# Raw rows one piece behind each context, values ahead of gates, two gate buffers and own columns for the squares of queries

## What is computed

```
xc = silu(causal_depthwise_conv(rmsnorm(x), 4 taps))
q, k = l2norm(xc @ wq), l2norm(xc @ wk)      16 heads of 16
v, beta, alpha = xc @ wv, sigmoid(xc @ wb), sigmoid(xc @ wa + 4)
for each token t:  S = alpha S;  S = S + k (beta (v - S k));  o = S q
h = x + o @ wo;  hn = rmsnorm(h);  x1 = h + (silu(hn @ wg) * (hn @ wu)) @ wd
cross attention of 256 queries over 120 context rows, 16 heads
mixture of 8 experts (one per token), three layers, exact GELU
```

## Time and profile before

| What | us |
|---|---|
| median of 3 runs (1851.98 to 1855.04) | 1852.46 |
| the profiled execution | 1856.45 |
| its span, first to last instruction | 1854.8 |
| VectorE busy in the span | 1229.1 |
| PE busy | 1378.5 |
| POOL busy | 1005.5 |
| ACT busy | 849.2 |

### The profile page before, as it was taken

The page is one execution under the profiler, slowest core; times in us unless marked ns, Lnnn a source line. Parts: engine busy times, 40 slices in busy tenths (PEclk is TensorE's granted clock), DMA queues, the critical chain, the costliest instruction groups (busy, mean ns, idle before and its releaser), DMA issues. The chain is left out here.

```text
span 1854.8 us, 33139 instructions
## 1 busy us (share of the span) xinstructions
PE 1378.5 (74%) x9256; PEld 1202.1 (65%) x9257; DVE 1229.1 (66%) x3269; ACT 849.2 (46%) x2808; POOL 1005.5 (54%) x1250
## 2 busy tenths in 40 slices
PE   6067748657047666565865899997499999999997
PEld 4055636436035555454654778886399999999997
DVE  3799899994988999999775143444344443443442
ACT  4332323326023675666876588887232332332332
POOL 4499789883779998999766334341112122112111
PEclk9578578859568888887977999998699999999999
DMA  5316012574121011000112111133130510511200
GB/s 131 75 41 137 17 36 59 145 169 94 63 85 33 23 34 34 22 23 27 28 34 81 54 50 45 55 121 127 37 102 24 166 34 23 166 35 47 75 17 7
DMA packets 183745, 119.32 MB, mean 64 GB/s; under 512 B 125745, under 2 KB 164584, under 8 KB 183144
## 3 DMA queue, kind: packets, MB, share of 16 engines
q1 hardware_dynamic: 119976, 90.98, 17.7%
q10 hardware_dynamic: 59248, 18.72, 4.1%
q0 software_dynamic: 4432, 8.60, 1.3%
HBM read 83.44 MB, written 35.74 MB: 64 GB/s over the span
## 5 line engine op out<-in xcount | busy, mean ns | idle before, releaser
L247 POOL TENSOR_TENSOR wt<-wt 128x1024 f32<-128x1024 f32 x128 | 301.4, 2355 | 72.4 <-DVE wt L192 51.4
L253 POOL TENSOR_TENSOR wt<-wt 128x512 f32<-128x512 f32 (+2 forms) x384 | 304.4, 793 | 30.1
L1972 PE MATMUL e_ph<-e_g,e_w 128*128 128x128 f32 x2496 | 285.2, 276 | 0.7 <-ACT e_g L1942 0.7
L1972 PEld LDWEIGHTS e_ph<-e_g,e_w 128*128 128x128 f32 x2496 | 281.9, 192 | 0.9 <-issue 0.9
L192 DVE SCALAR_TENSOR_TENSOR wt<-wt,scan 128x256 f32<-128x256 f32 x512 | 242.9, 474 | 1.8 <-POOL wt L247 1.8
L171 DVE TENSOR_REDUCE wt<-wt 128x16 f32<-128x272 f32 x512 | 220.2, 430 | 0.1
L182 DVE TENSOR_TENSOR scan<-wt,scan 128x256 f32<-128x256 f32 x512 | 215.9, 422 | 0.3
L160 DVE TENSOR_TENSOR wt<-wt,scan 128x256 f32<-128x256 f32 x512 | 211.0, 412 | 0.9 <-PEq L270 0.5
L1450 ACT ACTIVATE wt<-p_pX,p_mx 128x120 f32<-128x120 f32 x512 | 176.4, 387 | 75.8 <-DVE p_mx L1235 75.6
L1933 ACT ACTIVATE e_g<-e_ph,wt 128x128 f32<-128x128 f32 x156 | 48.7, 363 | 305.0 <-PE e_ph L1972 305.0
L1851 POOL TENSOR_TENSOR e_ve<-e_mv,eps 128x1 f32<-128x1 f32 x39 | 7.4, 189 | 330.8 <-DVE e_mv L1907 330.8
(11 more groups left out here) (229 smaller groups left out, 2884.9 us busy)
## 6 DMA issues: line engine op xcount, KB each, us to landing
wt<-in_L_ffn_W SPq DMA_DIRECT2D x24, 1024.0 KB, 5.2
qkv<-f_st ACTq DMA_DIRECT2D x48, 256.0 KB, 2.6
p_kE<-kE SPq DMA_DIRECT2D x16, 480.0 KB, 3.7
p_vP<-vP SPq DMA_DIRECT2D x16, 480.0 KB, 4.6
wt<-qkv SPq DMA_DIRECT2D x12, 512.0 KB, 5.3
e_xt<-routed ACTq DMA_DIRECT2D x39, 130.0 KB, 2.1
f_xt<-in_x SPq DMA_DIRECT2D x32, 128.0 KB, 2.9
p_oT<-o SPq DMA_DIRECT2D x16, 256.0 KB, 2.8
```

What stands on the lines that cost most here:

```text
L247: nc.gpsimd.tensor_tensor(x, s["S"][:, h, z * Q:(z + 1) * Q], s["qn"][:, h, z * Q:(z + 1) * Q].rearrange("p t (o d) -> p t o d", o=1).to_b ...
L253: nc.gpsimd.tensor_tensor(x[:, :, :, 0:half], x[:, :, :, 0:half], x[:, :, :, half:2 * half], ALU.add).then_inc(s["o_fold"][h], 1)
L1972: ins = nc.tensor.matmul(ph2[:, c // 2, c % 2], w2[:, s, i, c * P:(c + 1) * P], g1[:, i], start=(i == 0), stop=(i == C1 - 1))
```

## The change

Five edits, all in `front_and_scan`:

- `bst` gets two slots by the unit's parity, with a semaphore each; a copy of gates waits for the store of two units before.
- `load_raw` loads values ahead of gates, and can load one of the four pieces alone.
- In the loop over contexts, the four whole `load_raw` behind contexts 2, 4, 6, 8 become 16 pieces, one behind each of steps 1 to 16: keys, queries, values, gates of part 2 half 0, then part 3 half 0, part 2 half 1, part 3 half 1.
- Where the span is 64 columns (parts 0 and 1), the squares of queries get columns 64 to 127 of `squares`, and keys keep 0 to 63; ACT then waits for the sums of the half before only.
- `with_lengths` takes places among the 16 steps of two chunks: behind steps 6, 8, 9, 12, 14, 15 for part 1 and 5, 8, 9, 11, 14, 15 for parts 2 and 3, where it was 4, 6, 7, 12, 14, 15 for both.

```diff
-        bst = sb("bst", [48, 4, PT])
+        bst = sb("bst", [48, 2, 4, PT])
...
+        plane = lambda i, n: squares[:, :, i * n:(i + 1) * n] if 2 * n <= TB else squares[:, :, 0:n]
...
-                for i, name, dst in ((1, "k", x["k"]), (0, "q", x["q"]), (3, None, None), (2, "v", x["vo"])):
+                for i, name, dst in ((1, "k", x["k"]), (0, "q", x["q"]), (2, "v", x["vo"]), (3, None, None))[some.start:some.stop]:
                     if i == 3:
                         later = part > 0
-                        sp.wait_ge(gates_out[later], 128 * (units - U * later))
+                        for slot in range(2):
+                            sp.wait_ge(gates_out[later][slot], 64 * (units - U * later))
...
-            later = {2 + 2 * i: (2 + i % 2, i // 2) for i in range(4)}
+            later = {1 + i: (2 + i // 4 % 2, i // 8, range(i % 4, i % 4 + 1)) for i in range(16)}
...
                 def sums(i):
                     folds = (p * 2 + i) * 4
                     dve.wait_ge(sq_done, p * 2 + i + 1)
+                    x = plane(i, n)
...
-                        dst = squares[:, 0:half, 0:n] if half > 1 else lens[:, h, i:i + 1, 0:n]
-                        nc.vector.tensor_tensor(dst, squares[:, 0:half, 0:n], squares[:, half:2 * half, 0:n], ALU.add).then_inc(fold_done, 1)
+                        dst = x[:, 0:half] if half > 1 else lens[:, h, i:i + 1, 0:n]
+                        nc.vector.tensor_tensor(dst, x[:, 0:half], x[:, half:2 * half], ALU.add).then_inc(fold_done, 1)
...
-            def with_lengths(some, c, last=False):
-
-                for h in range(2):
-                    parts = list(lengths(some, h))
-                    for u in range(R):
-                        scan_step(nc, dve, s, 0, c + h, u, last=last and h == 1)
-                        if u in (4, 6, 7):
-                            parts.pop(0)()
+            def with_lengths(some, c, places, last=False):
+
+                parts = [*lengths(some, 0), *lengths(some, 1)]
+                for u in range(2 * R):
+                    scan_step(nc, dve, s, 0, c + u // R, u % R, last=last and u >= R)
+                    if u in places:
+                        parts[places.index(u)]()
...
-            with_lengths(1, CHUNKS // 2 - 3)
+            with_lengths(1, CHUNKS // 2 - 3, (6, 8, 9, 12, 14, 15))
...
-            with_lengths(2, CHUNKS - 2, last=True)
+            with_lengths(2, CHUNKS - 2, (5, 8, 9, 11, 14, 15), last=True)
...
-                if n == U:
-                    act.wait_ge(gates_out[0], n * 128)
-                elif n >= 1:
-                    act.wait_ge(gates_out[n > U], (n - U * (n > U)) * 128)
-                nc.scalar.activation(bst[:].rearrange("p b t -> p (b t)"), pp[0:48, 3, 0], ACT.Copy).then_inc(evac_done, 1)
+                if n >= 2:
+                    later = n - 2 >= U
+                    act.wait_ge(gates_out[later][n % 2], ((n - 2 - U * later) // 2 + 1) * 128)
+                nc.scalar.activation(bst[:, n % 2].rearrange("p b t -> p (b t)"), pp[0:48, 3, 0], ACT.Copy).then_inc(evac_done, 1)
...
-                    if p < 2 and (p or i):
-                        act.wait_ge(fold_done, (p * 2 + i) * 4)
-                    elif p == 2 and i == 0:
-                        act.wait_ge(fold_done, 16)
-                    elif p >= 2:
+                    if p in (1, 2):
+                        act.wait_ge(fold_done, ((p - 1) * 2 + i + 1) * 4)
+                    elif p == 3:
+                        act.wait_ge(lens_done, summed(p - 1, i))
+                    elif p > 3:
                         act.wait_ge(lens_done, summed(p, i) - 1)
-                    nc.scalar.activation(squares[:, :, 0:n], src[:, h, :, now], ACT.Square).then_inc(sq_done, 1)
+                    nc.scalar.activation(plane(i, n), src[:, h, :, now], ACT.Square).then_inc(sq_done, 1)
...
-                        ins = nc.tensor.matmul(squared[:, i, 0:n], ident[:], squares[:, d, 0:n], start=(d == 0), stop=(d == HD - 1))
+                        ins = nc.tensor.matmul(squared[:, i, 0:n], ident[:], plane(i, n)[:, d], start=(d == 0), stop=(d == HD - 1))
```

More of the change, by code:

```diff
@@ L317, in front_and_scan @@
         out = [sem(f"f_out_{n}") for n in "qkv"]
-        gates_out = [sem(f"f_gates_out{i}") for i in range(2)]
+        gates_out = [[sem(f"f_gates_out{i}{slot}") for slot in range(2)] for i in range(2)]
         (ss_done, rstd_done, xn_done, T_done, tail_done, xT_done, conv_done, xc_done, proj_done, evac_done) = (
@@ L349, in store_gates @@
                         eng.dma_start(k["gates"][i, n, a, g].rearrange("q h t -> h q t"),
-                                      bst[32 * i + g * H // G:32 * i + (g + 1) * H // G, 2 * a:2 * a + 2]).then_inc(gates_out[n >= U], 16)
+                                      bst[32 * i + g * H // G:32 * i + (g + 1) * H // G, n % 2, 2 * a:2 * a + 2]).then_inc(gates_out[n >= U][n % 2], 16)
         @block.sync
@@ L371, in load_weights, with load_raw @@
                     sp.dma_start(bv[:], row(w["L0_xattn_bv"], 1)).then_inc(small_in, 16)
-            def load_raw(part, h):
+            def load_raw(part, h, some=range(4)):
                 units = U * part + U // 2 * (h + 1)
```

## The result

The changed kernel takes 1829.59 us (median of 4 runs, 1825.32 to 1832.96) against 1853.44 for the kernel before (4 runs on the same chip): a ratio of 0.988, with a 95% interval of 0.9861 to 0.9899. That is 23.9 us, 1.3%, faster. The profiled execution took 1832.96 us, its span is 1831.3.

The account below looks back on a forecast made before the run. VectorE's scan and its two waits for ACT's sigmoid were taken to bound the first stage. Gains of 3.6 + 5.9 + 20.2 = 29.7 us off 1856.45 gave 1826.7, less 4.0 for the median 1822.7; range 1817 to 1834, about 0.8.

Parts of the forecast that it names:

- the forecast's band of 1 to 7: VectorE's second wait for gates: 1 to 7 us left, time 1821 to 1827, chance 0.40.
- Rival 4: First-stage gains do not reach the end, as something else holds the barrier or second stage: 1852.5 us, chance 0.04.
- Start: Ahead of VectorE's scan: second gates buffer and own columns for squares start it 3.6 us earlier, bounds 5.5 and -1.
- The 1.5 us charged for values ahead of gates: SP's loads ahead of the scan: gates going behind the values costs about 1.5 us again.
- First stall: VectorE's 5.93 us wait for part 1's sigmoid: own columns or later place alone covers it; 5.9 gained, bounds 5 and 5.9.
- Second stall: VectorE's 23.16 us wait at gates of parts 2 and 3: 20.2 us gained, 3 left; bounds 23.2 and 3.
- 20.6 us saved: Loop of sixteen contexts ends at 420.0 instead of 440.6; 26 saved at PE's fast pace, 14 at the slow.
- contexts over in 75 to 82 us: A sign that would show the forecast: ACT's sixteen contexts last 75 to 82 us.
- Rival 1: Both VectorE stalls vanish and the scan alone bounds the first stage: 32.7 us gained, 1819.8, chance 0.33.
- the sum's last line: 29.7 us off the profiled execution's 1856.45 gives 1826.7; the median lies 4.0 below the profiled one, so 1822.7.
- Rival 2: Context loop hardly shortens; second stall keeps 8 to 20 us, gain 12.5 to 24.7, time 1828 to 1840, chance 0.19.
- Rival 3: Context loop becomes serial, each load waiting for its piece: about 161 us instead of 96.3, time 1905, chance 0.04.

Follow-up runs that it names:

- shared_columns: Changed kernel with squares of queries in the keys' columns again, with the waits this needs, new places kept; 1829.41 us.
- late_place: Changed kernel with VectorE's parts for parts 2 and 3 behind steps 8, 10, 11, 13, 14, 15; 1822.94 us.
- warm_pe: Changed kernel with eight more PE products of 128 columns behind each context, whose result nobody reads; 1824.09 us.
- changed_again: The changed kernel without an edit, run and profiled a second time; 1829.75 us.
- gates_first: Changed kernel with gates loaded ahead of values in every group again; 1828.86 us.
- spread_alone: Kernel before with only the raw-row pieces spread one by one over the contexts, gates still ahead of values; 1840.96 us against 1854.21.
- part2_early: Changed kernel with part 2's raw rows loaded behind units 13 and 14, leaving eight pieces of part 3 in the context loop; 1825.32 us.

## Why the prediction was right, and where its terms were off

It said faster, 1822.7 us, 1817 to 1834; measured were 1829.59, inside the range and 6.9 above the number. A stall of 6.5 and 5.3 us is in the forecast's band of 1 to 7; the median is not in its 1821 to 1827. Point by point:

- **That VectorE's chain arrives whole at the barrier** holds: 26.95 us at the barrier from 4.11 + 5.93 + 16.65 = 26.7 at the three places. The 396.2 to 398.8 us of scan show it for every run. Rival 4, that the time doesn't reach the end, is out.
- **Start, 3.6 us:** 4.11, and 2.6 to 4.2 over the eight profiles. The second buffer brings it, as the term said; own columns, in the same term, bring nothing (60.84 in `shared_columns` too). The 1.5 us charged for values ahead of gates were 0.5 in this profile, no more than the spread.
- **First stall, 5.9 us:** 5.93. "Either alone covers" it is half wrong. The places alone do; the columns alone leave 2.74 us at the roots, which the step left at two steps behind the gates without asking what was late next.
- **Second stall, 20.2 us gained:** 16.65, and 17.9 in the second execution. This is the mis-sized term, and in it the loop's length: "20.6 us saved" from a pace between PE's two; it was 13.3, near the figure for the slow pace, and 17.3 in the second. (That figure is given as 14; its own steps, 9 x 5.5 + 3 x 4.8 = 63.9, make it 15.1. And 23.16 - 2.96 - 20.6 + 1.8 + 0.9 leaves 2.3 us, where 3 were taken.) The row that it was built on showed a granted clock of 0.71, and the changed loop has 0.75 over its length; the slow end was the one nearest to the row. The rest came out as charged or better: the place and the later arrival gave 5.0 us (2.96 expected; the contexts start 12.9 us sooner, VectorE comes to its place only 7.9 sooner), and the sums on PE and sigmoid cost 1.6 more (1.8). By these, 23.2 - 5.0 - 13.3 + 1.6 = 6.5. The sign "contexts over in 75 to 82 us" was missed by the first execution (83.1) and met by the second (79.1).
- **Rival 1**, no stall left, 1819.8: this is what `late_place` and `warm_pe` are, 1822.94 and 1824.09. So some 3 us of the miss seem to lie outside the stalls, in the sum's last line; in the changed kernel, too, the three places give 26.7 us and the medians 22.9 to 23.9. It took a gain read from one execution off the median of others. The profiled pair, before and `late_place`, differs by 31.7 us (1856.45 - 1824.77), near the 32.7 that the rival's sum gives; the medians by 29.5. The profiled execution of before lay 4.0 above its median, and part of that was, it seems, in the very stalls that the sum took out. That was not tried by itself.
- **Rival 2**, that the loop hardly shortens, is wrong in its reason (13 to 17 us shorter), though its lower edge, 8 us of stall, lay near.
- **Rival 3**, the serial loop of 161 us, did not come: SP issued the next load ahead of the stores, and the loop took 83.1. By the same row a context load does stand behind its piece: the median landing is 4.9 us, against 4.7 with a piece and 2.9 without.

PE's waits for context loads were to spread "over a dozen contexts of 1 to 3 us each". They are still 8, up to 4.7, with a sum of 19.7 instead of 35.1; the sum fell by 15.4, and the loop by 13.3. In these waits PE stands idle, and behind the one of 4.22 us shown above the granted clock was 0.50, where it was 1.00 ahead of it. The Trainium skill (TensorE: Matmul & The Clock Gate, section HAM oscillation — how this bites in real kernels) tells of a kernel whose groups of products are shorter than the wait for their data, so that each starts slow. The trace agrees at that wait, 2.8 us of products and 4.22 of waiting; but only 8 of the 16 contexts have a wait. Over 60 us of the loop the clock was 0.72 with the waits, and 1.00 when the gaps were filled.

What stays open: why the same loop took 83.1 us in one execution and 79.1 in another, and 76.8 to 83.7 where the edits lay elsewhere. Of the nine profiles with the pieces spread one by one and no added products, the shortest loop has the highest granted clock, 0.81 (above), and the longest the lowest, 0.71, `shared_columns`:

```profile
331.90:415.60 83.70, 65.41 (x254) 46.54 (x254) 83.70 (x258) 36.47 (x113) 73.44 (x75) 0.71 0.74 180
```

In between the two do not go together: 0.75 with 83.1 us in the changed kernel, 0.76 with 79.1 in `changed_again`, and 0.77 with 83.5 in `gates_first` and in `spread_alone`, the two with gates ahead of values. That a higher clock shortens the loop is shown by `warm_pe`; what sets the clock one way or the other from one execution to the next was not found.

## What to carry to other kernels

A wait that stops the bounding engine can be hidden by asking later: three more scan steps ahead of it did as much as a supplier that is done sooner (`part2_early`); the scan ended at 458.9 and 457.4 where it was 463.4, and with both together no sooner, at 457.8. The first takes one line. Before a wait is removed, ask what the same engine needs next; here it was the roots. And bulk loads that share a queue with small ones that a loop needs each step go one behind each step: the same bytes, in pieces, made the loop 13 us shorter.

## What the runs showed that was not expected

- Adding work to PE made a loop faster: 128 products that nobody reads took 79.1 to 83.1 us of contexts down to 75.7, with the granted clock at 1.00 instead of 0.72 to 0.74 from 340 to 400 us.
- In `warm_pe` a context takes 4.7 us (75.7 by 16), at a DMA share of 0.94 and with PE busy 59.70 of 60 us: the transfers or the added products themselves can be the next bound there, and no run tells which. The clock is not all: with eight pieces instead of sixteen (`part2_early`) the contexts took 69.4, with no product added and a granted clock of 0.85, below the 0.97 that `warm_pe` has over its loop.
- SP's issue of a context load took 0.4 to 1.6 us in the loop of the kernel before, and 0.46 to 3.40 in the changed kernel, 335 to 405 us (count, then shortest, median and longest in ns):

```profile
L411 SPq DMA_DIRECT2D f_acc<-in_ctx x13: 460/1694/3399, 337.9 to 402.2; - x13
```

  Behind a gates piece it took 0.46 to 0.52, behind a large piece 1.57 to 3.40: a load behind a large piece costs SP time in the issue itself, and what stands behind it on SP waits meanwhile.
